# Another string of 985 steps for a two-layer transformer block in one kernel

## The reference, cut to what matters

```python
x = x + 0.5 * int8_ffn(layernorm(x))      # part 0: quantise, 128x128 matmul, scale, bias
x = x + attention0(layernorm(x))          # part 1: 16 heads of 8, rope, causal
x = x + 0.5 * int8_ffn(layernorm(x))      # part 2
x = x + 0.5 * gated_ffn(layernorm(x))     # part 3: silu(x wg) * (x wu) @ wd, hidden 384
x = x + attention1(layernorm(x))          # part 4: 16 heads of 64, causal
x = x + 0.5 * gated_ffn(layernorm(x))     # part 5
```

## Time and profile before

| | before |
|---|---|
| median of 3 runs | 794.64 us (791.90 to 794.64) |
| the profiled execution | 794.18 us |
| its span (first to last instruction) | 792.4 us |
| steps 0 to 399 | 36.0 to 286 us |
| steps 400 to 984 | 286 to 761 us |
| behind the string | 761 to 792.4 us |

### The profile page before, as it was taken

The page is one execution under the profiler, slowest core; times in us unless marked ns, Lnnn a source line. Parts: engine busy times, 40 slices in busy tenths (PEclk is TensorE's granted clock), DMA queues, the critical chain, the costliest instruction groups (busy, mean ns, idle before and its releaser), DMA issues.

```text
span 792.4 us, 21544 instructions
## 1 busy us (share of the span) xinstructions
PE 724.7 (91%) x9387; PEld 431.6 (54%) x9387; DVE 534.4 (67%) x739; ACT 454.5 (57%) x534; POOL 466.6 (59%) x367
## 2 busy tenths in 40 slices
PE   2767888888888899999999999999999999999997
PEld 1633445444444554566556566555666555656774
DVE  7598888889998685668775675655655565453337
ACT  2325667889775779555646545555534656646202
POOL 6726446125542300489979849885861898877530
PEclk9756899999999999999999999999999999999999
DMA  8000000000000000001101101100110110111100
GB/s 272 2 1 2 3 2 3 2 4 2 2 3 2 2 2 3 2 3 29 28 3 29 29 2 31 27 10 24 29 29 2 29 29 2 29 29 30 29 27 27
DMA packets 13226, 16.20 MB, mean 20 GB/s; under 512 B 3053, under 2 KB 10573, under 8 KB 13133
## 3 DMA queue, kind: packets, MB, share of 16 engines
q1 hardware_dynamic: 12556, 14.50, 6.5%
q10 hardware_dynamic: 576, 0.33, 0.1%
HBM read 13.26 MB, written 1.17 MB: 18 GB/s over the span
## 4 chain that ended last, share of the span: by engine, by line
PE 74%; DVE 12%; ACT 9%; issue 3%; POOL 1%; DMA 1%; ACTq 0%; DVEq 0%; POOLq 0%
PE ps L1261 19%; PE ps L1210 17%; DVE big L1074 7%; ACT Pr L697 7%; PE ps L1181 6%; PE ps L1425 5%; PE ps L1240 5%; PE ps L1464 3%; PE ps L1432 3%; PE ps L1382 2%; PE ps L1271 2%; PE ps L1376 1%; PE ps L1251 1%; PE ps L1231 1%; PE ps L1221 1%
## 5 line engine op out<-in xcount | busy, mean ns | idle before, releaser
L697 ACT ACTIVATE Pr<-ps,exp_scale 128x1024 f32<-128x1024 f32 (+1 forms) x285 | 277.4, 1029 | 132.4 <-PE ps L1261 68.9
L679 POOL TENSOR_TENSOR V0s<-V0s,Pr 128x1024 f32<-128x1024 f32 x77 | 181.3, 2354 | 92.6 <-PE ps L1210 65.1
L1105 DVE TENSOR_REDUCE mxb<-ps 128x8 f32<-128x1024 f32 (+1 forms) x154 | 173.7, 1151 | 85.0 <-PE ps L1261 55.4
L1074 DVE TENSOR_REDUCE big<-ps 128x8 f32<-128x1024 f32 (+1 forms) x164 | 171.3, 1089 | 27.7 <-PE ps L1240 20.1
L1261 PE MATMUL ps<-big 64*128 64x128 f16 (+2 forms) x2560 | 171.0, 260 | 0.2 <-ACT Pr L697 0.2
L1240 PE MATMUL ps<-big 32*128 32x128 f16 (+2 forms) x1280 | 103.7, 279 | 34.8 <-DVE big L1074 16.1
L1261 PEld LDWEIGHTS ps<-big 64*128 64x128 f16 x2560 | 92.6, 94 | 76.9 <-issue 28.8
L1210 PE MATMUL ps<-Pr,V1s 128*64 128x128 f32 (+2 forms) x960 | 112.8, 372 | 0.1
L1240 PEld LDWEIGHTS ps<-big 32*128 32x128 f16 x1280 | 43.5, 96 | 108.5 <-ACT Pr L697 40.3
L679 POOL TENSOR_TENSOR acts<-acts,Pr 128x1024 f32<-128x1024 f32 x35 | 83.2, 2378 | 22.2 <-PE ps L1210 10.8
L1181 PE MATMUL ps<-Pr,V0s 128*18 128x128 f32 (+2 forms) x1280 | 80.8, 380 | 0.0
(11 more groups left out here) (242 smaller groups left out, 920.5 us busy)
## 6 DMA issues: line engine op xcount, KB each, us to landing
rec_b<-scratch_dram SPq DMA_DIRECT2D x30, 256.0 KB, 3.9
X<-in_x_dram SPq DMA_DIRECT2D x2, 256.0 KB, 3.5
big<-in_pick_rows_dram SPq DMA_DIRECT2D x2, 256.0 KB, 3.5
X<-in_x_dram SPq DMA_DIRECT2D x1, 512.0 KB, 5.9
rec_b<-in_w_q_dram SPq DMA_DIRECT2D x1, 512.0 KB, 6.1
XT<-in_w_k_dram SPq DMA_DIRECT2D x1, 512.0 KB, 6.8
XT<-in_w_v_dram SPq DMA_DIRECT2D x1, 512.0 KB, 7.9
wo_s<-in_w_o_dram SPq DMA_DIRECT2D x1, 512.0 KB, 8.5
```

Source lines behind the costliest of these rows:

```text
L679: g.tensor_tensor(dst, dst, src, ALU.add).then_inc(summed, 1)
L697: ins = a.activation(dst[:, part], src, func, scale=scale)
L1074: ins = v.tensor_reduce(maxima_of(mall[:, r, 2 * u:2 * u + 2][:, part], i), block_view(src, i), AX.X, ALU.max, negate=True)
L1105: ins = v.tensor_reduce(maxima_of(mxb[:, r][:, part], arg), block_view(src, arg), AX.X, ALU.max, negate=True)
```

## The change

Only the string differs, all twelve of its rows but nothing around it. Its first row and its last:

```diff
-    "ammmmmmmmammmmmmmmmmmhhmamtememememhwhemewmemwememwmememwehmhmehehmwwemtheeewmhememwmemwemegemwemmhm"
+    "ammmmmmmmammmmmmmmmamtmmehemehmhmememememmmweehmwemmwemwemewemehwmehewemhthweaemehweemwegemehwmemwemm"
...
-    "EWEMMWEMMWEEEEEhVWSTWWWWMEEMWMWEMMWWMEEEMWSEEEEMWWWWThhhWWEEEEWEEEOhOEWWWWSEOhhOhWWWW"
+    "WMEWMEEhKVWEMhQTWWWMEEEhWESEMEWWWWMEEEMWWSMEMWWMEEEEWWMMhTVWWWEEEEWWWOSEEEEEOOOWWWWWW"
```

More of the change, by code:

```diff
@@ L185 @@
 ORDER = (
-    "ammmmmmmmammmmmmmmmmmhhmamtememememhwhemewmemwememwmememwehmhmehehmwwemtheeewmhememwmemwemegemwemmhm"
[L187 to L194, removed]
-    "EWEMMWEMMWEEEEEhVWSTWWWWMEEMWMWEMMWWMEEEMWSEEEEMWWWWThhhWWEEEEWEEEOhOEWWWWSEOhhOhWWWW"
+    "ammmmmmmmammmmmmmmmmamtmmehemehmhmemememmmweehmwemmwemwemewemehwmehewemhthweaemehweemwegemehwmemwemm"
+    "emwemwmehmewmmhmemhmewmeemetmmhmhmwhhmmhmememwmeegemwememhhwmmehhhewemwaemwememwhemmhetmwemememwmeme"
+    "mwmeewmememwemamewemewemetmemwemwemewmegemehwmemwmegeamhmmhehewewemmemhhwemewehmhewemmewemmemtwemmam"
+    "mwheehwemmewheehwemewememewmhemwememewemheegthhhwhhhwememwmmheewmemheewemewhmeewmememwmemwemwemhweme"
+    "mQQtKKVgeeMwMeVMeweMeweMeweMewMeeweMgewMeeweeTKQwwMMgEVEMWMEMWMEMWMEEhMEMhEMWhEMWTKQWWWMEMhWhMEEMWWh"
+    "MEEMSMWWMEMWMEEEMWMTQhMKWWWMEMVSMEEMWEMMWWWMEEEWMEEhTKQhWWWWMEEEhVWhhMEMWMEWMEMWMMSWTEMEWMEEQKhWWMMW"
+    "EMhhWEMWTEMMWEEMWhVhShWWMEEEhQWWEMMWEMEWKTEWWMEhhVSEMEWhMMMWWWMEEEWWMEEMWMEEEEhWWWWQVKTVSMEEMWWEMMWW"
+    "MEMWMEEEEQKWWMEEMSMEMWTMWWWMMKQWWMEEEEWWEMMWWEMSMEMWTEMWMEMWWMEMWMEEMVQKVOSMMOMEEEMWWWWMEEEKQTOOhVME"
+    "WWWhMMMWWMETSMEEEEMWWWWMEEEMWEMQVKhWWWMMWMEMWTSMEEEEEMWWMEEEWMMQVKMMWWWWhhWEEEEEMWMMMWWWMEWMSEThWWEM"
+    "WMEWMEEhKVWEMhQTWWWMEEEhWESEMEWWWWMEEEMWWSMEMWWMEEEEWWMMhTVWWWEEEEWWWOSEEEEEOOOWWWWWW"
 )
```

## The result

The changed kernel took **786.55 us** in the median of five runs (783.86 to 788.05), the kernel before 792.1 beside it. The ratio is 0.9918 with a 95% interval of 0.9888 to 0.9947, so it is faster by 0.8%, some 6.5 us (5.6 between the two medians). A second measurement gave 0.9939 (0.9907 to 0.9970). The forecast was 793.7 and no change that can be told; the time lies at the lower edge of the range, and on the side to which the text gave a chance of 0.22.

What follows compares the result with a forecast made beforehand. Bound by TensorE's own work from 286 to 761 us, by three engines' balance and waits in steps 0 to 399. -3.5 + 2.8 - 0.5 + 0.5 = -0.7 us from 794.18, plus 0.2, gave 793.7 us; range 786.5 to 802.

Steps and rivals of the forecast that it cites:

- The pair stage: Steps from 286 to 761 us: TensorE 99.6% busy, order saves nothing, late GpSimd additions may lose; +0.5 us (0 to 3).
- The balance of steps 0 to 399: First 400 steps: work of TensorE, VectorE and ScalarE lies more evenly; -3.5 us (-1 to -6.2).
- the new waits: Steps 0 to 399: five places where the new order makes engines wait more or less; together +2.8 us (0 to 7).
- around step 400: Near step 400: one exponential and one weigh of TensorE's leave the fully busy stretch; -0.5 us (-1 to +0.5).
- xq of batch 1: Part 0, steps 0 to 399: waits for GpSimd's rounding, with seven maxima as cover instead of nine; +1.0 us.
- The turn of group 1: Steps 0 to 399: stands one place further from its last maxima, so waits less; -0.5 us.
- The turn of group 2: Steps 0 to 399: VectorE's closing falls beside GpSimd's rope operations and is held up; +1.5 us (0 to 3.2).
- R1: Rival, faster: balance gain in full (-6.2) and a half-clock stretch at 92 us gone (-4.0); 786.8 us, chance 0.22.
- R2: Rival, slower: TensorE starves at two chains in steps 0 to 399, bringing another half-clock stretch; 800.7 us, chance 0.17.
- R3: Rival: GpSimd's additions come late at one to three places; +2 to +4 us, about 797, chance 0.11.
- Behind the string: After the last step: same list of work, and the last addition still has time to spare; 0 us.
- steps 400 to 984 shorter than 470 us: Sign named in advance: this stretch taking under 470 us would show the prediction wrong.

Runs made afterwards that it cites:

- e1: Kernel before up to step 399, then the new string's order from step 400 on; 0.9961 of the time of the kernel before.
- e2: New string up to step 399, then the order of the kernel before from step 400 on; 0.9972 of the time of the kernel before.
- e8: Kernel before with weighs, maxima's and exponentials' scores rearranged behind step 400 for fewer form changes and bank waits; 1.0024 of the time of the kernel before.
- e5: Kernel before plus bare products behind its end, alone and alternated; float16 score and float32 weigh products alternated took 0.24 us more a round; whole time no measure.
- e7: Kernel before with 27 weighs behind step 400 each swapped with the maximum's scores behind it, 104 weigh stretches kept; 1.0079 of the time of the kernel before.
- e10: The new string unchanged, run once more beside two rearranged strings; 0.9939 of the time of the kernel before.

## Why the prediction was wrong, step by step

**The pair stage** was the step that failed. It said: "With TensorE busy for 99.6% the order can save nothing there", and put the term at +0.5, 0 to 3. Measured: -4.5 in the two profiles, -3.8 by e1 with the same 6056 products. A busy engine was taken for a constant amount of work. But the time of TensorE's own work depends on what stands beside what: one step of the same kind costs 0.86 or 1.01 us by what precedes it, and the new order has 263 changes of form instead of 290, at 0.13 us each. The prediction gave each kind of step one price, and the changes none.

**The balance of steps 0 to 399**, -3.5, and **the new waits**, +2.8. Together with -0.5 around step 400 the forecast for this part was -1.2. The two profiles show -1.6; over six profiles each, before's first 400 steps took 245.2 to 252.6, mean 248.8, the new ones 244.4 to 251.7, mean 247.0, which is -1.8; e2's runs say -2.2 in the mean against before beside them. So the sum was about right, with a spread that hides its parts. VectorE's own work, which was to shrink by about 4 us, went from 213.57 to 211.48. The other parts were not right either:

- *xq of batch 1* didn't wait, where +1.0 was forecast. The peak starts at 76.05, later than before, and GpSimd's rounding ends at 83.96 + 1.90 = 85.86; xq starts at 86.59, 0.73 us later, straight behind an exponential's scores.

```profile
76.05 1.21 DVE L1024 TENSOR_REDUCE stats<-D 128x8 f32<-128x1024 f32 x1
...
83.96 1.90 POOL L632 TENSOR_TENSOR ffn_g<-ffn_h,magic_s 128x1024 f16<-128x1024 f32 x1
...
86.59 0.62 PE L1340 MATMUL ps<-idh_s,ffn_g 128*128 128x128 f16 x8
```

  Seven maxima for VectorE were counted as all the cover; TensorE had exponentials and weighs of its own there.
- *The turn of group 1*: its whole wait of 1.49 us is gone, not 0.5 of it. It stands 8 steps behind its last maximum now, where before it was 5; the prediction counted one place.
- *The turn of group 2* was to wait 1.5 us longer, since VectorE's closing would fall beside GpSimd's rope. It does fall there, as forecast, and the wait went from 1.47 down to 0.65:

```profile
118.22 2.35 POOL L651 TENSOR_TENSOR V1s<-V1s,turns 128x1024 f32<-128x1024 f32 x1
...
119.85 0.76 DVE L1080 TENSOR_SCALAR big<-big 128x32 f16<-128x32 f32 x1
...
120.64 0.19 DVE L1081 SCALAR_TENSOR_TENSOR big<-big 128x32 f16<-128x32 f32 x1
120.65 2.39 POOL L652 TENSOR_TENSOR V1s<-V1s,big 128x1024 f32<-128x1024 f32 x1
120.98 0.22 PE L1404 MATMUL ps<-idh_s,big 128*64 128x128 f16 x1 [0.65 <-DVE big L1081]
```

  L1080 is held until L651 ends at 120.57, but L1081 starts at 120.64, ahead of L652, and takes 0.19. The price of this meeting was what was left of one operation, not one for each instruction of the chain. The sum had taken, where both were held, for the rule; the two took 0.95 us together, and over 2 were named as a sign.
- *Exponentials*: 33 waits and 11.7 us instead of 20 and 8.8, which no term spoke of. The longest wait that the list puts down to a maximum is 1.9 us instead of 1.2, but it isn't a new one: it stands ahead of group 0's first exponentials, where before waited 2.9, put down to L1066. Before and after:

```profile
65.95 0.61 PE L1240 MATMUL ps<-big 32*128 32x128 f16 x8 [2.90 <-DVE big L1066]
```

```profile
63.87 0.61 PE L1240 MATMUL ps<-big 32*128 32x128 f16 x8 [1.93 <-DVE big L1074]
```

**R1, the faster one**, was right in direction for a reason that is hardly its own. The stretch at half clock from 92 us has gone, as it said:

```profile
92.00:102.50 10.50, 9.22 (x176) 5.09 (x174) 8.36 (x21) 10.21 (x12) 7.15 (x11) 1.00 0.01 3
200.00:220.00 20.00, 17.43 (x245) 8.81 (x241) 16.92 (x18) 12.11 (x14) 14.19 (x20) 0.76 0.01 2
```

But another stands at 200 to 220 us with a clock of 0.76, where before had 1.00, and the mean clock of the new kernel's runs is lower, not higher. That the measured time, 786.55 us, comes within 0.3 of R1's 786.8 is luck: its two terms, -6.2 in the first part and -4.0 by the clock, are not what was gained, and the 3.8 us of the second part were in neither. **R2** didn't happen: no wait of its two lasted. **R3** didn't either in the new string, in which no wait of TensorE for GpSimd shows behind step 400; e8 shows that the spare was indeed small. **Behind the string** 31.48 us against 31.42 with the same cut, as forecast.

What the prediction named as proof against itself, "steps 400 to 984 shorter than 470 us", came out at 470.65, so that it wasn't met, by 0.65 us: the line was drawn too low for the 3.8 us that a saving by order was worth. That the time lies inside the range, by 0.05 us, is luck too.

## What to carry to other kernels

An engine that is busy all the time is bound by its work only at the price that its order gives: look up one kind of step behind different neighbours before writing that an order can save nothing. On TensorE, products that use the array in the same form are cheaper side by side, 0.13 us for each change saved here; but a step that needs no bank also gives the others time to empty theirs, and moving 27 of them by one place cost 4.9 us. How far merging pays isn't shown, since the two strings that went furthest had their banks dealt anew. When an experiment is to change one thing, compare what else the program derives from it, here the banks and the counts of instructions. And where a kernel's time follows its granted clock, compare kernels at equal clock, or with many runs, before a few us are put down to an order.

## What the runs showed of the hardware that was not expected

- A change between forms of the array costs 0.10 to 0.17 us, for products of 512 columns in a row without a pause (e5): 64 rows to 64 columns 0.11 (float16) to 0.12, 64 rows to the whole array 0.11 to 0.15, 64 columns to the whole array 0.12 to 0.17. A change of type within one form costs nothing measurable (-0.02 us a round).
- The control e7: 27 weighs one place later, with nearly the same changes (292 and 290) and the same banks, cost 4.9 us of waits.
- A clock mean lower by 0.01 goes with 4.2 to 5.6 us in this kernel. It comes nearly all from ahead of step 400, since the clock from there to the end of the string is 1.00 in every trace; e10 and the first profile of the same string differ by 3.5 us there (251.7 and 248.2) with second parts of 470.66 and 470.65.
